# Last four tiles in buffers of their own, end units' rows posted ahead of a root, list rows read in pairs

## What is computed

```python
x = layernorm(x + attn(x))            # quantised linear layers, 16 heads
x = layernorm(x + xattn(ctx, x))      # cross attention over ctx_1024
x = layernorm(x + ffn(x))             # mixture of 8 experts, top 2

def ffn(tgt):                         # the block that the change is in
    logits = einsum('bsd,ed->bse', tgt, Wr) + br
    top_v, top_i = top_k(logits, 2)
    router_w = sum(one_hot(top_i, 8) * softmax(top_v)[..., None], axis=-2)
    h = relu(einsum('bsd,efd->bsef', tgt, W1) + b1)      # F = 512
    o = einsum('bsef,edf->bsed', h, W2) + b2
    tgt2 = einsum('bsed,bse->bsd', o, router_w)
    return layer_norm(tgt + tgt2) * gamma + beta         # then the outer layernorm
```

## Time and profile before

| | us |
|---|---|
| median of 3 runs | 725.49 |
| lowest, highest | 724.27, 726.21 |
| span of the profiled execution | 767.7 |
| busy in it: PE | 613.9 (80%) |
| busy in it: DVE | 557.7 (73%) |
| busy in it: POOL | 479.1 (62%) |
| busy in it: ACT | 476.2 (62%) |

### The profile page before, as it was taken

How to read it: one execution, slowest core, us unless ns; L and a number is a source line. 1 busy time by engine, 2 the same in 40 slices (tenths; PEclk the granted TensorE clock), 3 DMA queues, 4 the chain that set the end, 5 groups by cost and what they waited for, 6 DMA issues and landing times.

```text
span 767.7 us, 19357 instructions
## 1 busy us (share of the span) xinstructions
PE 613.9 (80%) x6308; PEld 528.3 (69%) x6308; DVE 557.7 (73%) x1699; ACT 476.2 (62%) x975; POOL 479.1 (62%) x655
## 2 busy tenths in 40 slices
PE   2578999999897779999999999987877889888300
PEld 0367887788896568888888878876755677777300
DVE  4998999999955676878878787955546355567665
ACT  4675888888745567777676767754242344457434
POOL 6277877778863555446777776835347445467753
PEclk9699999999999599999999999999978799999855
DMA  6611211212234334433110100002211222351141
GB/s 181 191 17 19 26 22 24 24 24 22 37 81 151 136 127 150 175 138 134 35 34 18 30 18 25 18 24 61 58 60 58 81 71 67 98 160 52 49 137 55
DMA packets 113107, 55.39 MB, mean 72 GB/s; under 512 B 70625, under 2 KB 103841, under 8 KB 113025
## 3 DMA queue, kind: packets, MB, share of 16 engines
q1 hardware_dynamic: 103984, 25.46, 15.0%
q10 hardware_dynamic: 4496, 19.02, 6.3%
q0 software_dynamic: 4544, 9.84, 3.7%
HBM read 21.25 MB, written 33.05 MB: 71 GB/s over the span
## 4 chain that ended last, share of the span: by engine, by line
PE 53%; DVE 15%; issue 12%; ACT 10%; another core or an unknown queue 3%; POOL 3%; DMA 3%; SPq 1%; ACTq 0%; DVEq 0%; POOLq 0%
PE PS L1194 14%; PE PS L991 10%; PE PS L1102 5%; PE PS L1112 4%; DVE PS L1911 3%; PE PS L1302 2%; PE PS L1161 2%; PE PS L1283 2%; PE PS L1300 2%; PE PS L1285 1%; PE PS L1301 1%; DMA W_raw<-in_L_ffn_W_dram 1%; DVE W_raw L2287 1%; PE PS L1284 1%
## 5 line engine op out<-in xcount | busy, mean ns | idle before, releaser
L991 PE MATMUL PS<-prod,ident 128*128 128x144 f32 x1024 | 137.1, 294 | 8.7 <-DVE hctx L1891 8.4
L991 PEld LDWEIGHTS PS<-prod,ident 128*128 128x128 f32 x1024 | 131.4, 195 | 16.5 <-issue 9.3
L1194 PE MATMUL PS<-W_raw 128*72 128x128 f32 x1024 | 131.0, 284 | 8.5 <-issue 4.5
L760 POOL TENSOR_TENSOR prod<-prod,v 128x2048 f32<-128x2048 f32 x32 | 117.5, 3673 | 31.0 <-ACT prod L1397 31.0
L1194 PEld LDWEIGHTS PS<-W_raw 128*72 128x72 f32 x1024 | 117.3, 149 | 14.0 <-issue 7.5
L880 POOL DMA_INDIRECT ys<-W_raw,ids x78 | 77.3, 991 | 63.5 <-ACT W_raw L1635 40.4
L2174 DVE TENSOR_REDUCE m<-PS 128x8 f32<-128x1024 f32 x64 | 77.9, 1218 | 43.5 <-PE PS L1112 43.5
L2287 DVE SCALAR_TENSOR_TENSOR W_raw<-PS,W_raw 128x512 f16<-128x512 f32 x78 | 52.1, 688 | 66.4 <-ACT W_raw L1619 35.4
L820 POOL DMA_INDIRECT xs<-Y,spot_u x64 | 64.3, 1005 | 26.4 <-issue 15.0
L1911 DVE TENSOR_REDUCE PS<-pair_sq 128x128 f32<-128x1024 f32 x64 | 75.0, 1218 | 0.0
L1553 ACT ACTIVATE W_raw<-PS 128x1024 f32<-128x1024 f32 x64 | 65.8, 1028 | 14.1 <-remote 10.7
(11 more groups left out here) (321 smaller groups left out, 1548.5 us busy)
## 6 DMA issues: line engine op xcount, KB each, us to landing
xs<-pad ACTq DMA_DIRECT2D x16, 1152.0 KB, 4.5
Y<-xs SPq DMA_DIRECT2D x39, 144.0 KB
W_raw<-ys SPq DMA_DIRECT2D x16, 256.0 KB
W_raw<-in_L_ffn_W_dram SPq DMA_DIRECT2D x1, 2048.0 KB
shuffle<-hctx SPq DMA_DIRECT2D x32, 64.0 KB, 3.0
Y<-shuffle SPq DMA_DIRECT2D x32, 64.0 KB, 1.8
cs<-in_ctx_dram SPq DMA_DIRECT2D x8, 256.0 KB
out_dram<-W_raw SPq DMA_DIRECT2D x8, 256.0 KB, 2.9
```

The lines of the kernel that those rows point to most:

```text
L760: pool.tensor_tensor(rows[:, :, 0:D].rearrange("p t (d h) -> p t d h", d=HD), a.broadcast_to((P, H, HD, H)), v.broadcast_to((P, H, HD, H)) ...
L991: last = pe.matmul(PS[:, 6, 0:TC], ident[:], prod2[:, i % 2, TC * t:TC * (t + 1)], start=(t == 0), stop=(t == H - 1))
L1194: last = pe.matmul(PS[0:HO, 7, a * P:(a + 1) * P], v_frame[:, i % 2, a, HO * n:HO * (n + 1)], PT[:, i % 2, 8 * a + n, :], start=(n == 0), ...
```

## The change

Three things change.

1. Tiles 4 to 7 get `zb` and `yb` of their own, in `pair_sq`. `load_rows` no longer waits for `stored`, and SP loads tiles 4 to 7 one after the other, before it stores tiles 2 to 7.
2. On POOL, `center(3)` leaves the loop over units. Its root comes behind the last send, its beta add behind the root of tile 2 (`finish(2)`). On DVE, tile 2's statistics and joining come ahead of `center(3)`, and `finish(2)` ahead of `scale_rows(3)`.
3. `load_unit` puts rows 2p and 2p + 1 of the unit into partition p, where they were p and p + 128.

```diff
-        zb = [rows2[:, NT * n:NT * (n + 1)].rearrange("p (i d) -> p i d", i=TB) for n in range(4)]
-        yb = [rows2[:, NT * n:NT * (n + 1)].rearrange("p (i d) -> p i d", i=TB) for n in range(4, 8)]
+        late = pair_sq[:].rearrange("p a b -> p (a b)")
+        zb = [home[:, NT * n:NT * (n + 1)].rearrange("p (i d) -> p i d", i=TB) for home in (rows2, late) for n in range(4)]
+        yb = [home[:, NT * n:NT * (n + 1)].rearrange("p (i d) -> p i d", i=TB) for home in (rows2, late) for n in range(4, 8)]
...
-                sp.dma_start(xu[j % XD], xs[bass.ds(row, U), :].rearrange("(s p) r -> p s r", p=P)).then_inc(unit_in[j % XD], 16)
+                sp.dma_start(xu[j % XD], xs[bass.ds(row, U), :].rearrange("(p s) r -> p s r", s=2)).then_inc(unit_in[j % XD], 16)
...
                 n = t % 4
-                if t >= 4:
-                    sp.wait_ge(stored[n], 16)
-                for a, buffer in enumerate((zb[n], yb[n])):
+                for a, buffer in enumerate((zb[t], yb[t])):
...
-            for t in range(4, 6):
+            for t in range(4, T):
                 load_rows(t)
-            for t in range(2, 4):
-                store_tile(t)
-                load_rows(t + 4)
-            for t in range(4, T):
+            for t in range(2, T):
                 store_tile(t)
...
+            def invert_third(t):
+
+                invert(t, ve3, rstd3, ve3_ready, rstd3_ready)
+
             def center(t):
 
-                invert(t, ve3, rstd3, ve3_ready, rstd3_ready)
+                invert_third(t)
                 add_beta(t)
...
                 t, n = divmod(j - FIRST_FINAL + 1, FINAL_STEP)
-                if 0 <= t < EARLY and n == 0:
+                if 0 <= t < EARLY - 1 and n == 0:
                     center(t)
...
+            invert_third(EARLY - 1)
             finish(EARLY - 2)
+            add_beta(EARLY - 1)
             finish(EARLY - 1)
...
-            center(EARLY - 1)
             fourth_stats(EARLY - 2)
             join_fourth(EARLY - 2)
+            center(EARLY - 1)
+            finish(EARLY - 2)
             scale_rows(EARLY - 1)
-            finish(EARLY - 2)
             finish(EARLY - 1)
```

More of the change, by code:

```diff
@@ L609, in store_tile @@
                 sp.wait_ge(o4_ready, t + 1)
-                sp.dma_start(out[TB * t:TB * (t + 1)].rearrange("b s d -> s b d"), zb[t % 4]).then_inc(stored[t % 4], 16)
+                sp.dma_start(out[TB * t:TB * (t + 1)].rearrange("b s d -> s b d"), zb[t]).then_inc(stored[t % 4], 16)
             for t in range(FULL - 2, FULL):
@@ L1642, in normalise @@
                 for i in range(TB):
-                    last = act.activation(zb[t % 4][:, i, :], zb[t % 4][:, i, :], ACT.Identity, bias=shift3[:, t % 4, i:i + 1],
+                    last = act.activation(zb[t][:, i, :], zb[t][:, i, :], ACT.Identity, bias=shift3[:, t % 4, i:i + 1],
                                           scale=rstd3[:, t % 4, i:i + 1])
@@ L1650, in normalise_again @@
                 for i in range(TB):
-                    last = act.activation(zb[t % 4][:, i, :], zb[t % 4][:, i, :], ACT.Identity, bias=shift4[:, t % 4, i:i + 1],
+                    last = act.activation(zb[t][:, i, :], zb[t][:, i, :], ACT.Identity, bias=shift4[:, t % 4, i:i + 1],
                                           scale=rstd4[:, t % 4, i:i + 1])
@@ L2292, in add_second @@
             def add_second(t):
-                z = zb[t % 4]
+                z = zb[t]
                 dve.wait_ge(yrow_in[t % 4], 16 * 2 * (t // 4 + 1))
-                step(dve.tensor_tensor(z, z, yb[t % 4], ALU.add))
+                step(dve.tensor_tensor(z, z, yb[t], ALU.add))
             def add_input(t):
-                z = zb[t % 4]
+                z = zb[t]
                 settle()
@@ L2307, in third_stats @@
                 need(dve, n3_ready, t - 3)
-                row_stats(zb[t % 4], bn3[:, t % 4])
+                row_stats(zb[t], bn3[:, t % 4])
             def join_third(t):
@@ L2343, in fourth_stats @@
                 need(dve, o4_ready, t - 3)
-                row_stats(zb[t % 4], bn4[:, t % 4])
+                row_stats(zb[t], bn4[:, t % 4])
             def join_fourth(t):
```

## The result

| | median, us | lowest to highest | ratio to before, 95% interval |
|---|---|---|---|
| before | 725.49 | 724.27 to 727.15 | |
| after | 721.94 | 721.10 to 723.11 | 0.9951 [0.9934, 0.9969] |

A forecast was written before the change was run, and what follows sets the result against it. VectorE's order of work, with two load waits, was taken to bound the tail. Gains of 1.44 (tile 4 earlier), 2.21 (own buffers) and 0 (list rows) made 3.65 us: 725.49 to 721.8 us, range 720.2 to 725.1.

The forecast's parts named there:

- both stalls: VectorE's waits for loads before the first adds of tile 4 (2.89 us) and tile 6 (1.47 us).
- Part 1, posts: GpSimd's last four posts directly follow unit 36's, ending at 724.25 instead of 728.07: 3.8 us earlier.
- The second pair begins near 722.0, past 721.65, so nothing holds it: Unit 38's posts on GpSimd: its rows are ready at 721.65, before the posts begin, so they do not wait.
- Rival (c): Post of unit 38: late rows hold the posts; decides at 3.9 us later; up to 0.8 us slower, 726.3; chance 0.04.
- a wait of unit 38's posts for ScalarE: Sign of being wrong, on GpSimd: unit 38's posts wait for ScalarE's rows; no size given.
- Part 1, tile 3 moved back: Tile 3's root follows the posts; tile 4's first add on VectorE starts at 731.77, before 733.21: 1.44 us gained.
- Rival (b): Tile 3's shift on VectorE is blocked by tile 2's root: 0.6 us later, gain 3.05, 722.4 us; chance 0.08.
- The second gain is 1.54 + 0.67: Tile 6's first add: own buffers remove the load wait (1.54) and the beta add's slowdown (0.67), 2.21 us.
- (e): List loads: paired rows bring their upper bound or thin out the queue, 1.9 us more, 719.9; chance 0.06.
- Rival (a): VectorE's load waits are shorter without the profiler: gain only 0.4 to 1.1 us, 724.4 to 725.1; chance 0.18.
- (d): Loads of the four tiles share the queue: tile 4 in at 733.6 at worst, 2.2 us gain remains, 723.7; chance 0.04.
- a GpSimd root under tile 6's first add: Sign of being wrong, in the tail: a GpSimd root or beta add runs under tile 6's adds, forecast at 0.69.

The follow-up runs named there:

- root_between: Against the changed kernel: tile 3's root between the posts of units 37 and 38, beta add behind the last post, scale_rows(3) before finish(2); 721.42 us, ratio 0.9946.
- root_again: root_between run once more, its kernel unchanged, on the same chip as a repeat of the changed kernel; 721.28 us, ratio 0.9942 to before.

## Why the prediction held, point by point

- **The forecast in all.** 3.65 us forecast, 3.55 measured. At clock 1.00, the clock of the rows that the sum was made from, the tail fell from 51.3 (mean of two) to 47.9, by 3.4 us; at 0.50 by 2.4. The total agrees because the whole change removes both stalls, whichever part removes the second; the split between the parts was wrong. That the total agrees to 0.1 us is luck: the interval of the measurement is 2.2 to 4.8 us, and the forecast took no account of the second clock.
- **Part 1, posts.** Forecast: the last post ends 7.77 after the relu's start (at 724.25). Measured: 8.14 and 8.18 at clock 1.00, 9.22 at 0.50. The step that was mis-sized is "The second pair begins near 722.0, past 721.65, so nothing holds it": a margin of 0.35 us. Between ready rows and a post whose engine waits for them lie 0.75 us, not 0, so the post starts 0.4 late. And the margin was taken at one clock: at 0.50 the rows come 1.05 later. Ready at 6.25 plus 0.75 gives the 7.00 at which that post begins.
- **Rival (c)** had the right place, the post of unit 38, but asked 3.9 us of delay before it decided for slower. What came was about 1.1 us in some executions, so the kernel is faster in every profile. The change itself did not delay the rows: after has both values. The recorded sign of being wrong, a wait of unit 38's posts for ScalarE, did come (an idle of 1.76 us in after; at clock 1.00 it is 0.66 and 0.71, against 0.30 between neighbouring posts).
- **Part 1, tile 3 moved back.** Last post's end to tile 4's add: 7.52 forecast, 7.45 and 7.46 in the three profiles of after. Its steps are in the rows above: the shift at 681.63 took 0.16 just behind the start of the second root (680.56 plus half of 2.03), and finish(2)'s shift at 682.62 took 1.22 and ended with the beta add.
- **Rival (b)**, a root that blocks the shift, falls by that 0.16, and by a VectorE add of 512 elements in root_between that took its usual 0.69 (683.08) beside a root that ran from 682.98 to 684.02. The rule of the Trainium skill, "SBUF — State Buffer", "Who interferes with whom", by which it would have been blocked until the root is through, is not what the rows show for a root of four elements per partition; for the beta add (1.22) they agree with it.
- **Part 2.** 2.21 forecast on top of part 1's 1.44. Alone it brings 2.3 to 2.5; on top of part 1 the profiles show nothing (48.95 without, 48.99 with it, both at 0.50). The step that failed is "The second gain is 1.54 + 0.67": the time is right, but all of it was put down to the buffers, without asking what part 1 does to the same stall. The stall's chain begins at the tile loads, and part 1 issues those 2.4 us earlier at clock 0.50 (3.5 in the whole change at 1.00), with an interval between them and the store. At 0.50 part 1 alone leaves tile 4's add where it was (16.68), and all its 2.4 us are the second stall's; at 1.00 the whole change brings tile 4's add 1.1 us forward (1.44 forecast) and tile 6's another 1.6, and that add then takes 0.7 less: 3.4 in all.
- **Part 3.** 0 forecast, a ratio of 1.0001 measured; (e) falls. **Rival (a)** falls by 2.91 and 1.46 in a span of 722.6; **(d)** by the 5.11 us.
- **Smaller things.** Another recorded sign of being wrong came too, a GpSimd root under tile 6's first add (693.84, 1.46 us, in after); it cost the add nothing (0.68), and the prediction's own working had put tile 5's root there. The eight loads took 5.2 to 5.7 us to issue and not about 4; nothing waited for that. The chances added up for "faster" make 0.72 and not 0.71.

One thing stays open: what decides between 0.50 and 1.00 over the last 26 products. The same kernel shows both. The slow clock stood in one of five profiles with GpSimd's old order and in six of nine with the new ones, too few to tie it to the order. Each of the three chips of the experiments showed both. No run was made that holds it still. What the unprofiled runs had is not seen either.

## What to carry to other kernels

When two edits attack stalls on one chain, ask for each stall what remains of it once the other edit is in; two gains read from one trace may be the same gain. Where an engine's own order hid how late its input is, moving its work forward ends at the input: count the time from a released wait to the start (0.75 us here), and take the input's time at the slower clock as well. And the wait that then appears is a place for work that must be done anyway, as the root between the posts shows.

## What the runs showed of the hardware

A long GpSimd two-input operation can cost VectorE more than the operation's own length. This is VectorE in root_again, a gamma product that takes 0.68 elsewhere:

```profile
680.95 2.45 DVE L2334 TENSOR_TENSOR W_raw<-W_raw,gam 128x512 f32<-128x512 f32 x1 [1.71 <-ACT W_raw L1646]
```

It began 0.6 us ahead of the beta add at 681.56, during a post (680.58 to 681.54), and ended 0.56 us after it (682.84). That is 1.8 us lost to an add of 1.28, by GpSimd's spans, which are rough. A post alone does no such thing: in root_between the same product began at 680.22, ran beside a post (680.35 to 681.75), was through before the beta add, and took 0.69. Why the product in root_again made no use of the time ahead of the add was not tried. In the other direction, a GpSimd root in after that began while VectorE was in tile 5's first add (690.82 to 691.50) took 1.38 us instead of 1.02:

```profile
690.99 1.38 POOL L882 TENSOR_TENSOR rstd<-ve,half 128x4 f32<-128x4 f32 x1 [3.13 <-DVE ve L1873]
```
